# Four of sixteen scan inputs by GpSimd from broadcast rows, their decay in PSUM, and TensorE's sums behind its other jobs

## The chip, the cores and the metric

The kernel runs on one core of a Trainium2 chip. The metric is the time of one execution on the device in microseconds (us). Before the change the runs took 4894.6, 4897.47 and 4899.58 us, median 4897.47.

## The reference, cut to what matters

A layer norm, a selective state-space block with a residual, a second layer norm, and a gated feed-forward block whose activations and weights are rounded to a four-bit grid in blocks of 16. Input is 16 sequences of 1024 tokens with 256 features. The part that the change touches is the scan:

```
delta = softplus(dt_proj(dt_r) + bias)          # per head, 128 channels
A = -exp(A_log)                                 # 16 states per channel
def step(s, inp):
    d_t, u_t, B_t, C_t = inp
    dA = jnp.exp(d_t[..., None] * A)
    s = s * dA + (d_t * u_t)[..., None] * B_t[:, :, None, :]
    y_t = jnp.einsum('bhdn,bhn->bhd', s, C_t)
```

There are 4 heads with 128 channels and 16 states. B_t and C_t are the same for all channels of a head, so for each state one row of 512 tokens must be spread over 128 partitions.

## The kernel before, in words

**Tiling.** A unit is one head and 512 tokens (CH): two chunks of four heads per sequence, 128 units in all. Channels lie on the partitions and tokens along the free dimension. A unit is 16 steps, one for each state n. In units of a sequence's second chunk the scan starts from `carry`, otherwise from zero. Around the scans of unit u each step also does some job of other units: projections and convolution of units to come ("pre"), the first layer norm ("norm"), and the feed-forward part of 128-token tiles long past ("post").

**Order.** There is no planner at run time. Each engine runs `step(b, j, n)` for n = 0 to 15, and `due(job, slot)` puts a job in step slot % 16 of a unit that is slot // 16 units later than the job's start. Engines meet only through counting semaphores. Within a step the order of the code is the order of the engine's queue.

**The scan, state by state.** TensorE's `spread_b` (L904) writes the B row of state n, spread over 128 partitions, into one of three PSUM banks `db`; it does so in step n-2 and waits until the bank's last scan, three states ago, is over. VectorE multiplies the bank in place by `du` = delta*u (L840) in step n-1, ahead of the scan of state n-1, and runs the scan itself in step n (L852). ScalarE writes exp(delta*A) into the ring `decay` in SBUF (L440), five states ahead; in steps 4 and 5 it writes none and in step 6 three. GpSimd's `weigh` multiplies two states by two C rows (L629, one for each pair of states, in even steps); the C rows come from HBM by a broadcast DMA from SP's queue (`spread_c`, L383). TensorE adds the products of a pair into `ybank` and `cross` (`sum_up`, L919); the eight pairs are summed two at a time in steps 8, 12, 0 and 3 (`SUMS`).

**Jobs that the steps below name.** On TensorE: the residue matmuls L963 (step 0) and L967 (step 2), of which L963 waits for ScalarE's `hi` and `xdbl` (L553, L554, step 15); the transposes of h, L1007 (steps 13 and 0), and of v, L1051 (step 11); the gate matmuls L1026 (steps 2 and 4) and the up matmuls L993 (steps 3 and 5); the delta matmul L971 (step 4), which waits for ScalarE's `pieces` (L561); the down matmuls L1040 (steps 6, 7 and 8); the convolution L944. On ScalarE: the silu of the gate L495 (steps 3 and 5), the copy L520 of v's transpose (step 12), softplus L569 (step 5), the magnitude of h, L513 and L516 (steps 5 and 6), and table loads around silu and softplus. On VectorE: the gate product `gated` (L797, steps 4 and 6), the rounding of h, L787 and L790 (steps 6 and 7). On GpSimd: du (L655) in step 8, for the next unit.

**What of a step's queue order matters.** In each step TensorE runs the spread, then `sum_up`, then `side`, which holds all other jobs:

```python
                if g.within(STEPS):
                    spread_b(b, g)
                for slot, pairs in SUMS.items():
                    if w := due("scan", slot):
                        sum_up(w, pairs)
                side(b, u, due)
```

Of the kernel before, what the change touches and what calls it, by code (L numbers as in the profile page):

```python
# [52 lines left out]
AHEAD = RING - 1  # L53

DB_BANKS = 3
DB_BANK = [i % DB_BANKS for i in range(TRIP)]
DB_AGO = [next(d for d in range(1, TRIP) if DB_BANK[i - d] == DB_BANK[i]) for i in range(TRIP)]

# [4 lines left out]
C_RING = 4  # L63
# [68 lines left out]
def build(nc, hidden, win_t, conv_w, conv_b, xw, dtw, dt_b, a_log, dskip, wo_t, w_gate, w_up, w_down,  # L132
# [4 lines left out]
    with ExitStack() as ctx:  # L137
# [34 lines left out]
        cs = sb("cs", [C_RING, 2, CH])  # L172
        prod = sb("prod", [P_RING, 2, CH])
# [60 lines left out]
        c_landed = [sem(f"c_landed{i}") for i in range(C_RING)]  # L234
        decayed = sem("decayed")
        db_done = sem("db_done")
# [59 lines left out]
        c_rows = nc.dram_tensor("c_rows", (2, NST, CH), F32, kind="Internal").ap()  # L296

# [51 lines left out]
        def _(sp):  # L349
# [21 lines left out]
            free_reg = sp.alloc_register("free_count")  # L371
            rows_reg = sp.alloc_register("rows_count")

            def spread_c(b, u, p):

                slot = p % C_RING
                free = held(sp, free_reg, u.val(PAIRS, p + 1 - C_RING))
                if p == 0:
                    rows_in = held(sp, rows_reg, u.val(16, 16))
                    wait(sp, c_written, rows_in)  # L380
                wait(sp, weighted, free)
                rows = c_rows[u.mod(2), 2 * p:2 * p + 2, :].rearrange("n c -> (n c)")
                sp.dma_start(cs[:, slot, :, :].rearrange("p n c -> p (n c)"),  # L383
                             rows.unsqueeze(0).broadcast_to([P, 2 * CH])).then_inc(c_landed[slot], 16)

            def step(b, j, n):
                u, due = timetable(b, j, n)
                if v := due("pre", 18):
                    wait(sp, xd_evac, v.val(2, 2))
                    sp.dma_start(c_rows[v.mod(2), :, :], xdbl[64:64 + NST, :]).then_inc(c_written, 16)  # L390
                if n % 2:
                    p = (n + 5) // 2
                    w = u + p // PAIRS
                    if w.within(UNITS):
                        spread_c(b, w, p % PAIRS)
                if n == 2:
                    t_r = u + -4
                    if t_r.within(TILES):
                        wait(sp, x1_done, t_r.val(plus=-1))
                        sp.dma_start(xres[:, t_r.mod(2), :], x_tiles[t_r.val()]).then_inc(ld_res[t_r.mod(2)], 16)  # L400
                if n == 15:
                    t_x = u + 8
                    if t_x.within(TILES):
                        wait(sp, xn_done, t_x.val(plus=-1))
                        sp.dma_start(xin[:, t_x.mod(2), :], x_tiles[t_x.val()]).then_inc(ld_x[t_x.mod(2)], 16)
                    t_o = u + -8
                    if t_o.within(TILES):
                        wait(sp, o_done, t_o.val(plus=1))
                        sp.dma_start(out_tiles[t_o.val()], ot[:, t_o.mod(2), :]).then_inc(ot_free[t_o.mod(2)], 16)
# [14 lines left out]
        def _(act):  # L424
# [7 lines left out]
            def decays(b, j, n):  # L432
                g = Ix(b, j * NST + n, TRIP)
                if not g.within(STEPS):
                    return
                gu, gn = g.k // NST, g.k % NST
                if gn == 0:
                    wait(act, delta_done, Ix(b, gu, PER).val(plus=1))
                wait(act, scanned, g.val(plus=1 - RING))
                act.activation(decay[:, g.val() % RING, :], delta[:, gu % 2, :], ACT.Exp,  # L440
                               scale=aneg[:, gu % HEADS, gn:gn + 1]).then_inc(decayed, 1)

            def step(b, j, n):
                u, due = timetable(b, j, n)
                if t := due("norm", 19):
                    wait(act, xn_tp, t.val(plus=1))
                    wait(act, z_mm, t.div(4, 4, -4))
                    i = t.mod(4)
                    act.activation(xnt[:, t.mod(8) // 4, :, i * P:(i + 1) * P],
                                   bank_b[:, 0:DM].rearrange("p (k t) -> p k t", k=KM),  # L450
                                   ACT.Copy).then_inc(xnt_done, 1)
# [96 lines left out]
                if v := due("pre", 15):  # L548
                    wait(act, xd_mm, v.val(plus=1))
                    wait(act, dt_mm, v.val())  # L550
                    wait(act, res_mm, v.val(2))
                    wait(act, c_written, v.val(16))
                    act.activation(hi[:, :], pbank[:, :], ACT.Copy).then_inc(xd_evac, 1)  # L553
                    act.activation(xdbl[:, :], pbank[:, :], ACT.Copy).then_inc(xd_evac, 1)  # L554
# [3 lines left out]
                if v := due("pre", 19):  # L558
                    wait(act, res_mm, v.val(2, 2))
                    wait(act, b_spread, v.val(NST, -NST))  # L560
# [44 lines left out]
        def _(pool):  # L605
# [16 lines left out]

            def weigh(w, p):

                c, r = p % C_RING, p % P_RING
                wait(pool, scanned, w.val(NST, 2 * p + 2))
                wait(pool, c_landed[c], w.val(16 * PAIRS // C_RING, 16 * (p // C_RING + 1)))
# [4 lines left out]
            def step(b, j, n):  # L632
# [18 lines left out]
                if v := due("pre", 24):  # L651
                    wait(pool, delta_done, v.val(plus=1))
                    wait(pool, u_done, v.val(plus=1))
                    wait(pool, db_done, v.val(NST, -NST))
# [6 lines left out]
                if t := due("post", 46):  # L661
# [33 lines left out]
        def _(dve):  # L695
# [129 lines left out]
            def step(b, j, n):  # L825
# [8 lines left out]
                if g1.within(STEPS):  # L834
                    gu, gn = g1.k // NST, g1.k % NST
                    if gn == 0:
                        wait(dve, du_done, Ix(b, gu, PER).val(plus=1))
                    wait(dve, b_spread, g1.val(plus=1))
                    t = db[DB_BANK[g1.k % TRIP]]
# [3 lines left out]
                if g.within(STEPS):  # L843
                    h = u.mod(HEADS)
                    late = u.mod(PER) >= HEADS
                    wait(dve, decayed, g.val(plus=1))
                    wait(dve, db_done, g.val(plus=1))
# [4 lines left out]
                    dve.tensor_tensor_scan(state[:, n, :], decay[:, g.val() % RING, :], db[DB_BANK[g.k % TRIP]][:, :], start,  # L852
                                           ALU.mult, ALU.add).then_inc(scanned, 1)
# [29 lines left out]
        def _(pe):  # L883
# [3 lines left out]
            def step(b, j, n):  # L887
                u, due = timetable(b, j, n)
                g = Ix(b, j * NST + n + 2, TRIP)
                gu, gn = g.k // NST, g.k % NST  # L890
                if g.within(STEPS):
                    spread_b(b, g)
# [3 lines left out]
                side(b, u, due)  # L896

            def spread_b(b, g):

                gu, gn = g.k // NST, g.k % NST  # L900
                if gn == 0:
                    wait(pe, pieces_done, Ix(b, gu, PER).val(plus=1))
                wait(pe, scanned, g.val(plus=1 - DB_AGO[g.k % TRIP]))
                pe.matmul(db[DB_BANK[g.k % TRIP]][:, :], sel[:, gn, :], pieces[:, gu % 2, :],  # L904
                          start=True, stop=True).then_inc(b_spread, 1)
# [268 lines left out]
```

## Time and profile before

| | before |
|---|---|
| median of 3 runs | 4897.47 us (4894.6 to 4899.58) |
| the profiled execution | 4895.54 us, its span 4893.5 us |
| VectorE busy | 4549.8 us, 93% |
| TensorE busy (matmul) | 4234.6 us, 87% |
| ScalarE busy | 3509.2 us, 72% |
| GpSimd busy | 3429.2 us, 70% |
| spread matmuls L904 on TensorE | 690.1 us busy in the trace |
| products db*du L840 on VectorE | 1392.0 us, 2048 of them |
| scans L852 on VectorE | 2525.0 us, 2048 of them |

The times come from one profiled execution. A busy time adds up durations, and on VectorE and ScalarE the next instruction starts about 0.1 us before the one ahead is recorded as ended; where a step is priced, the distance from start to start is what counts. Matmul ends are modelled.

### The profile page before, as it was taken

How to read it: one execution, taken by the hardware profiler on the slowest of the kernel's cores; microseconds unless marked ns; L12 is line 12 of the kernel's file. 1: busy time of each engine (PE TensorE's matmuls, PEld its weight loads, DVE VectorE, ACT ScalarE, POOL GpSimd, SP SyncE). 2: the span in 40 equal slices, each digit the busy share in tenths (PEclk: the TensorE clock that was granted, in tenths of full speed). 3: DMA queues.
4: the chain of work that ended last, by engine and by line, in shares of the span. 5: the costliest groups of instructions: out<-in, count | busy, mean ns of one | idle time of the engine just before them, and what ended most of it. 6: DMA issues, size and time to landing. Idle time of an engine off the chain costs nothing. (4 is left out here: it accounts for less than half of the span.)

```text
span 4893.5 us, 64416 instructions
## 1 busy us (share of the span) xinstructions
PE 4234.6 (87%) x18927; PEld 1986.9 (41%) x19244; DVE 4549.8 (93%) x6828; ACT 3509.2 (72%) x5783; POOL 3429.2 (70%) x2321
## 2 busy tenths in 40 slices
PE   4788888888888888888898888888888888888887
PEld 1234444444444444444444444444444444444434
DVE  6999999999999999999999999999999999999994
ACT  3777777677777777777777777777777777777763
POOL 4777777777776777777777677777777677677763
PEclk8999999999999999999999999999999999999999
DMA  2333333333333333333333333333333333333330
GB/s 89 140 135 123 127 129 125 121 132 126 120 133 124 123 129 129 123 123 134 119 127 131 122 126 127 127 123 130 126 120 133 124 123 129 129 123 123 129 117 19
DMA packets 211138, 600.59 MB, mean 123 GB/s; under 512 B 25446, under 2 KB 76774, under 8 KB 210790
## 3 DMA queue, kind: packets, MB, share of 16 engines
q1 hardware_dynamic: 209088, 594.30, 35.6%
q8 instruction: 156, 2.56, 0.2%
q10 hardware_dynamic: 1702, 2.16, 0.2%
q14 instruction: 192, 1.57, 0.1%
HBM read 575.39 MB, written 20.97 MB: 122 GB/s over the span
## 5 line engine op out<-in xcount | busy, mean ns | idle before, releaser
L629 POOL TENSOR_TENSOR prod<-state,cs 128x1024 f32<-128x1024 f32 x1024 | 2416.5, 2360 | 1320.8 <-DVE state L852 1295.2
L440 ACT ACTIVATE decay<-delta,aneg 128x512 f32<-128x512 f32 x2048 | 1432.6, 717 | 925.3 <-DVE state L852 916.7
L840 DVE TENSOR_TENSOR db<-db,du 128x512 f32<-128x512 f32 x2048 | 1392.0, 680 | 56.7 <-PE db L904 55.5
L852 DVE TENSOR_TENSOR_SCAN state<-decay,carry,db 128x512 f32<-128x512 f32 x1024 | 1292.4, 1262 | 0.0
L852 DVE TENSOR_TENSOR_SCAN state<-decay,db 128x512 f32<-128x512 f32 x1024 | 1232.6, 1204 | 0.0
L904 PE MATMUL db<-pieces,sel 128*128 128x512 bf16 x1798 | 690.1, 386 | 393.5 <-DVE state L852 384.6
L919 PE MATMUL ybank<-prod,ident 64*64 64x512 f32 x4096 | 1003.4, 608 | 28.0 <-DVE hh L790 27.0
L919 PE MATMUL cross<-prod,ident 64*64 64x512 f32 x4096 | 1003.1, 609 | 0.0
L904 PEld LDWEIGHTS db<-pieces,sel 128*128 128x128 bf16 x2048 | 197.8, 97 | 1039.9 <-DVE state L852 809.0
L919 PEld LDWEIGHTS ybank<-prod,ident 64*64 64x64 f32 x4096 | 255.8, 134 | 455.1 <-issue 417.8
L1040 PE MATMUL bank_a<-wd,ht 128*128 128x256 f32 x1536 | 406.0, 389 | 3.2 <-DVE state L852 2.0
L1040 PEld LDWEIGHTS bank_a<-wd,ht 128*128 128x128 f32 x1536 | 283.1, 191 | 235.0 <-issue 210.8
L930 PE MATMUL pbank<-xnt,win 128*128 128x512 f32 x512 | 277.0, 624 | 103.7 <-ACT delta L569 64.1
L993 PE MATMUL bank_b<-wu,vt 128*128 128x352 f32 x1024 | 357.8, 472 | 0.0
L1026 PE MATMUL bank_a<-wg,vt 128*128 128x352 f32 x1024 | 347.4, 462 | 1.5 <-ACT hh L495 0.9
L797 DVE TENSOR_TENSOR hh<-hh,bank_b 128x352 f32<-128x352 f32 x256 | 132.5, 518 | 210.4 <-PE bank_b L993 203.1
L495 ACT ACTIVATE hh<-bank_a 128x352 f32<-128x352 f32 x256 | 118.6, 463 | 227.1 <-PE bank_a L1026 225.6
L1063 PE MATMUL bank_a<-wo,yg 128*128 128x256 f32 x1024 | 272.1, 391 | 0.4 <-ACT sz L546 0.3
L993 PEld LDWEIGHTS bank_b<-wu,vt 128*128 128x128 f32 x1024 | 184.3, 189 | 216.2 <-issue 160.0
L930 PE MATMUL bank_a<-xnt,win 128*128 128x512 f32 x512 | 261.0, 591 | 0.0
L944 PE MATMUL pbank<-xearly,cdiag 128*128 128x512 f32 x512 | 253.5, 598 | 3.4 <-ACT halo L531 1.5
L944 PE MATMUL pbank<-xlate,cdiag 128*128 128x512 f32 x512 | 251.1, 592 | 2.2 <-issue 0.5
(124 smaller groups left out, 6399.6 us busy)
## 6 DMA issues: line engine op xcount, KB each, us to landing
cs<-c_rows SPq DMA_DIRECT2D x1024, 512.0 KB, 3.6
xin<-in_hidden SPq DMA_DIRECT2D x128, 128.0 KB, 3.6
xres<-in_hidden SPq DMA_DIRECT2D x128, 128.0 KB, 3.4
out_x<-ot SPq DMA_DIRECT2D x128, 128.0 KB, 3.6
c_rows<-xdbl SPq DMA_DIRECT2D x128, 32.0 KB, 3.6
win<-in_win_t SPq DMA_DIRECT2D x1, 1024.0 KB, 10.6
state<-in_w_gate ACTq DMA_DIRECT2D x1, 704.0 KB
state<-in_w_up ACTq DMA_DIRECT2D x1, 704.0 KB
```

Source lines behind the costliest of these rows:

```text
L440: act.activation(decay[:, g.val() % RING, :], delta[:, gu % 2, :], ACT.Exp, scale=aneg[:, gu % HEADS, gn:gn + 1]).then_inc(decayed, 1)
L629: pool.tensor_tensor(prod[:, r, :, :], state[:, 2 * p:2 * p + 2, :], cs[:, c, :, :], ALU.mult).then_inc(weighted, 1)
L840: dve.tensor_tensor(t[:, :], t[:, :], du[:, gu % 2, :], ALU.mult).then_inc(db_done, 1)
L852: dve.tensor_tensor_scan(state[:, n, :], decay[:, g.val() % RING, :], db[DB_BANK[g.k % TRIP]][:, :], start, ALU.mult, ALU.add).then_inc(sc ...
L904: pe.matmul(db[DB_BANK[g.k % TRIP]][:, :], sel[:, gn, :], pieces[:, gu % 2, :], start=True, stop=True).then_inc(b_spread, 1)
L919: last = pe.matmul((ybank, cross)[k][c * Q:(c + 1) * Q, :], ident[rows, rows], prod[rows, p % P_RING, k, :], start=(p == 0), stop=(k == 1 ...
L930: return pe.matmul((pbank, bank_a)[part][:, :], win[:, k, part * DI + h * P:part * DI + (h + 1) * P], xnt[:, v.mod(8) // 4, k, :], start=( ...
L944: last = pe.matmul(pbank[:, :], cdiag[:, v.mod(HEADS), k, :], x[:, k:k + CH], start=(k == 0), stop=(k == TAPS - 1))
L993: last = pe.matmul(bank_b[:, 0:HALF], vt[:, k, :], wu[:, k, part * HALF:(part + 1) * HALF], start=(k == 0), stop=(k == KM - 1))
L1026: last = pe.matmul(bank_a[:, 0:HALF], vt[:, k, :], wg[:, k, part * HALF:(part + 1) * HALF], start=(k == 0), stop=(k == KM - 1))
L1040: last = pe.matmul(bank_a[:, 0:DM], ht[:, k, :], wd[:, k, :], start=(k == 0), stop=(k == KI - 1))
L1063: last = pe.matmul(bank_a[:, 0:DM], yg[:, t.mod(8) // 4, h, i * P:(i + 1) * P], wo[:, h, :], start=(h == 0), stop=(h == HEADS - 1))
```

## The change

- For states 1, 5, 9 and 13 (`BY_POOL`) the B row doesn't go over TensorE and PSUM. `xdbl`'s B rows are stored to HBM as `b_rows`, beside the C rows; SP's queue copies each of the four rows by a broadcast DMA into one of two buffers `brow` in SBUF (`copy_b`, steps 10, 14, 2 and 6); GpSimd multiplies it in place by du (`drive`, steps 15, 1, 5 and 11).
- For these states ScalarE writes the decay into the PSUM bank that TensorE doesn't use then, two states ahead, in place of the ring; the scan reads its factor from PSUM and its addend from SBUF. The other twelve states keep the old way, with a decay ring of six that runs six states ahead.
- TensorE's step is now spread, side, sums.
- The ring of C rows has three buffers, not four, and `spread_c` runs one pair less ahead.
- GpSimd computes du in step 13, not 8, and scales h (L664) in step 3, not step 14 of the unit before.

The core of the diff:

```diff
-AHEAD = RING - 1
+AHEAD = 6
+BY_POOL = (1, 5, 9, 13)
+WEIGHED_ROWS = 2
-C_RING = 4
+C_RING = 3
+            def copy_b(u, n):
+                g = u.val(NST, n)
+                i = of_pool(g)
+                if n == BY_POOL[0]:
+                    wait(sp, b_written, u.val(16, 16))
+                if i >= WEIGHED_ROWS:
+                    wait(sp, scanned, ON_POOL[i - WEIGHED_ROWS] + 1)
+                row = b_rows[u.mod(2), n:n + 1, :]
+                sp.dma_start(brow[:, i % WEIGHED_ROWS, :], row.broadcast_to([P, CH])).then_inc(b_landed[i % WEIGHED_ROWS], 16)
...
+                    sp.dma_start(b_rows[v.mod(2), :, :], xdbl[0:NST, :]).then_inc(b_written, 16)
...
+                for slot, k in ((10, 1), (14, 5), (18, 9), (22, 13)):
+                    if n == slot % NST:
+                        w = u + (1 - slot // NST)
+                        if w.within(UNITS):
+                            copy_b(w, k)
...
-                wait(act, scanned, g.val(plus=1 - RING))
-                act.activation(decay[:, g.val() % RING, :], delta[:, gu % 2, :], ACT.Exp,
-                               scale=aneg[:, gu % HEADS, gn:gn + 1]).then_inc(decayed, 1)
+                if gn in BY_POOL:
+                    wait(act, scanned, g.val(plus=1 - DB_BANKS))
+                    out, done = db[g.val() % DB_BANKS][:, :], decayed_psum
+                else:
+                    i = of_dve(g.val())
+                    if i >= RING:
+                        wait(act, scanned, ON_DVE[i - RING] + 1)
+                    out, done = decay[:, i % RING, :], decayed
+                act.activation(out, delta[:, gu % 2, :], ACT.Exp,
+                               scale=aneg[:, gu % HEADS, gn:gn + 1]).then_inc(done, 1)
...
+                if (n + 2) % NST in BY_POOL:
+                    decays(b, j, n + 2)
                 if n not in (4, 5):
                     for ahead in (AHEAD - 2, AHEAD - 1, AHEAD) if n == 6 else (AHEAD,):
-                        decays(b, j, n + ahead)
+                        if (n + ahead) % NST not in BY_POOL:
+                            decays(b, j, n + ahead)
...
+            def drive(w, n):
+                g = w.val(NST, n)
+                i = of_pool(g)
+                s = i % WEIGHED_ROWS
+                wait(pool, b_landed[s], 16 * (i // WEIGHED_ROWS + 1))
+                wait(pool, du_done, w.val(plus=1))
+                pool.tensor_tensor(brow[:, s, :], brow[:, s, :], du[:, w.mod(2), :], ALU.mult).then_inc(db_pool, 1)
...
-                if v := due("pre", 24):
+                if v := due("pre", 29):
...
+                for slot, k in ((-1, 1), (1, 5), (5, 9), (11, 13)):
+                    if w := due("scan", slot):
+                        drive(w, k)
-                if t := due("post", 46):
+                if t := due("post", 51):
...
+                    if n in BY_POOL:
+                        i = of_pool(g.val())
+                        wait(dve, decayed_psum, i + 1)
+                        wait(dve, db_pool, i + 1)
+                        by, plus = bank_g, brow[:, i % WEIGHED_ROWS, :]
...
-                if g.within(STEPS):
-                    spread_b(b, g)
+                if g.within(STEPS) and g.val() % NST not in BY_POOL:
+                    spread_b(g.val())
+                side(b, u, due)
                 for slot, pairs in SUMS.items():
                     if w := due("scan", slot):
                         sum_up(w, pairs)
-                side(b, u, due)
```

## Rows read from the trace of the kernel before

**Rows 1.** The page: busy time by engine, and TensorE's granted clock by slice.
```profile
PE 4234.6 (87%) x18927; PEld 1986.9 (41%) x19244; DVE 4549.8 (93%) x6828; ACT 3509.2 (72%) x5783; POOL 3429.2 (70%) x2321
...
PEclk8999999999999999999999999999999999999999
```

**Rows 2.** Groups of instructions by line: busy us, mean ns, idle before, releaser.
```profile
L840 DVE TENSOR_TENSOR db<-db,du 128x512 f32<-128x512 f32 x2048 | 1392.0, 680 | 56.7 <-PE db L904 55.5 <-remote 0.6
...
L655 POOL TENSOR_TENSOR du<-delta,uu 128x512 f32<-128x512 f32 x128 | 162.8, 1272 | 18.3 <-ACT delta L569 18.3
...
L508 ACT ACTIVATE bank_b<-v 128x256 f32<-128x256 f32 x128 | 47.1, 368 | 0.0
```

**Rows 3.** One line of the kernel, L748: count, durations, first and last start.
```profile
L748 DVE SCALAR_TENSOR_TENSOR yg<-uu,dsk,ybank x128: 733/739/747, 141.4 to 4793.1; 128x512 f32<-128x512 f32 x128
```

**Rows 4.** Timeline of VectorE, first and second half: start us, duration, line, [idle before].
```profile
2171.40 0.67 DVE L840 TENSOR_TENSOR db<-db,du 128x512 f32<-128x512 f32 x1
...
2175.29 0.52 DVE L797 TENSOR_TENSOR hh<-hh,bank_b 128x352 f32<-128x352 f32 x1 [1.50 <-PE bank_b L993]
...
2184.01 0.53 DVE L787 SCALAR_TENSOR_TENSOR hw<-cross,hh 128x352 f32<-128x352 bf16 x1 [0.21 <-ACT cross L516]
...
2185.58 0.50 DVE L790 SCALAR_TENSOR_TENSOR hh<-cross,hw 128x352 f32<-128x352 bf16 x1
...
2205.91 0.67 DVE L840 TENSOR_TENSOR db<-db,du 128x512 f32<-128x512 f32 x1
2206.50 0.17 DVE L744 BATCH_NORM_AGGREGATE mv<-stats 128x2 f32<-128x6 f32 x1
...
2207.69 0.67 DVE L840 TENSOR_TENSOR db<-db,du 128x512 f32<-128x512 f32 x1
...
2035.93 0.50 DVE L790 SCALAR_TENSOR_TENSOR hh<-cross,hw 128x352 f32<-128x352 bf16 x1
...
2058.67 0.67 DVE L840 TENSOR_TENSOR db<-db,du 128x512 f32<-128x512 f32 x1
```

**Rows 5.** Timeline of ScalarE in the same first-half unit.
```profile
2171.52 0.72 ACT L440 ACTIVATE decay<-delta,aneg 128x512 f32<-128x512 f32 x1 [0.51 <-DVE state L852]
...
2173.95 0.46 ACT L495 ACTIVATE hh<-bank_a 128x352 f32<-128x352 f32 x1
...
2177.55 0.46 ACT L495 ACTIVATE hh<-bank_a 128x352 f32<-128x352 f32 x1 [1.76 <-PE bank_a L1026]
...
2183.53 0.45 ACT L516 ACTIVATE cross<-hh 128x352 f32<-128x352 f32 x1
...
2195.40 0.38 ACT L520 ACTIVATE vt<-bank_b 128x256 f32<-128x256 f32 x1
...
2203.08 0.58 ACT L554 ACTIVATE xdbl<-pbank 128x512 f32<-128x512 f32 x1
```

**Rows 6.** Timeline of TensorE in that unit, neighbours of one line merged (xN).
```profile
2185.72 0.39 PE L904 MATMUL db<-pieces,sel 128*128 128x512 bf16 x1 [0.78 <-DVE state L852]
2186.34 0.65 PE L919 MATMUL ybank<-prod,ident 64*64 64x512 f32 x2 [0.23 <-DVE hh L790]
...
2188.21 1.13 PE L1040 MATMUL bank_a<-wd,ht 128*128 128x256 f32 x4
2189.18 0.38 PE L904 MATMUL db<-pieces,sel 128*128 128x512 bf16 x1
2189.40 2.95 PE L944 MATMUL pbank<-xearly,cdiag 128*128 128x512 f32 x6
...
2194.98 0.38 PE L1051 MATMUL bank_b<-ident,v 128*128 128x128 f32 x2
...
2204.41 0.49 PE L1007 MATMUL bank_b<-ident,hh 128*128 128x128 f32 x3 [0.16 <-issue]
2204.73 0.38 PE L904 MATMUL db<-pieces,sel 128*128 128x512 bf16 x1
```

**Rows 7.** DMA issues: count, KB each, median us to landing.
```profile
cs<-c_rows SPq DMA_DIRECT2D x1024, 512.0 KB, 3.6
```

More of the change, by code:

```diff
@@ L52, with of_dve, of_pool @@
 RING = 6
-AHEAD = RING - 1
+AHEAD = 6
 DB_BANKS = 3
-DB_BANK = [i % DB_BANKS for i in range(TRIP)]
-DB_AGO = [next(d for d in range(1, TRIP) if DB_BANK[i - d] == DB_BANK[i]) for i in range(TRIP)]
+BY_POOL = (1, 5, 9, 13)
+N_POOL = len(BY_POOL)
+N_DVE = NST - N_POOL
+WEIGHED_ROWS = 2
+ON_DVE = [g for g in range(STEPS) if g % NST not in BY_POOL]
+ON_POOL = [g for g in range(STEPS) if g % NST in BY_POOL]
+def of_dve(g):
+    return g // NST * N_DVE + sum(n not in BY_POOL for n in range(g % NST))
+def of_pool(g):
+    return g // NST * N_POOL + sum(n in BY_POOL for n in range(g % NST))
 PAIRS = NST // 2
-C_RING = 4
+C_RING = 3
 P_RING = 4
@@ L234, in build @@
         c_landed = [sem(f"c_landed{i}") for i in range(C_RING)]
+        b_written = sem("b_written")
+        b_landed = [sem(f"b_landed{i}") for i in range(WEIGHED_ROWS)]
+        db_pool = sem("db_pool")
         decayed = sem("decayed")
+        decayed_psum = sem("decayed_psum")
         db_done = sem("db_done")
@@ L833, in step @@
                 g1 = Ix(b, j * NST + n + 1, TRIP)
-                if g1.within(STEPS):
-                    gu, gn = g1.k // NST, g1.k % NST
+                if g1.within(STEPS) and g1.val() % NST not in BY_POOL:
+                    gu, gn = g1.val() // NST, g1.val() % NST
                     if gn == 0:
-                        wait(dve, du_done, Ix(b, gu, PER).val(plus=1))
-                    wait(dve, b_spread, g1.val(plus=1))
-                    t = db[DB_BANK[g1.k % TRIP]]
+                        wait(dve, du_done, gu + 1)
+                    wait(dve, b_spread, of_dve(g1.val()) + 1)
+                    t = db[g1.val() % DB_BANKS]
                     dve.tensor_tensor(t[:, :], t[:, :], du[:, gu % 2, :], ALU.mult).then_inc(db_done, 1)
@@ L851, in step @@
                     start = carry[:, h, n:n + 1] if late else 0.0
-                    dve.tensor_tensor_scan(state[:, n, :], decay[:, g.val() % RING, :], db[DB_BANK[g.k % TRIP]][:, :], start,
-                                           ALU.mult, ALU.add).then_inc(scanned, 1)
+                    dve.tensor_tensor_scan(state[:, n, :], by, plus, start, ALU.mult, ALU.add).then_inc(scanned, 1)
                 behind(b, j, n, due)
@@ L895, in step, with spread_b @@
                         sum_up(w, pairs)
[L896 to L900 removed]
+            def spread_b(g):
+                gu, gn = g // NST, g % NST
                 if gn == 0:
[L902 to L904 removed]
+                    wait(pe, pieces_done, gu + 1)
+                wait(pe, scanned, g + 1 - DB_BANKS)
+                pe.matmul(db[g % DB_BANKS][:, :], sel[:, gn, :], pieces[:, gu % 2, :],
                           start=True, stop=True).then_inc(b_spread, 1)
```

46 lines of the change are left out of this document (25 added, 21 removed).

## The prediction

> **What bounds the kernel now.** I read the busy shares first: VectorE is busy 93% of the span, TensorE 87%, GpSimd and ScalarE near 70% [rows 1]. So VectorE's work is what the change must shorten. Then the spacing of one instruction that runs once per unit (512 tokens of one head, 16 states): it starts 128 times from 141.4 to 4793.1 us, so a unit takes 4651.7/127 = 36.63 us, and 128 of them make nearly the whole span [rows 3]. The reader should see that anything worth x us per unit is worth 128x.
>
> Then one unit on each engine, in order of time. Two marks cut it. A is where VectorE starts the instruction behind scan 2, B where it starts the one behind scan 7. In the unit shown A is 2171.40, B is 2185.58, the next A 2207.69 [rows 4]: 14.18 us from A to B, 22.11 from B to A. In a unit of the second half of a sequence, whose scans are 0.06 longer, B to A is 22.74 [rows 4]. The two stretches have different limits:
>
> A to B is no VectorE stretch. VectorE waits 1.50 us before the first gate product (L797) and 0.21 before the rounding of the second half of h (L787) [rows 4]. What holds it is a chain over ScalarE and TensorE: the decay at 2171.52 waited for scan 2, and behind it in ScalarE's queue stand a table load and the first silu, which ends 3.0 us after A; ScalarE then waits 1.76 us for TensorE's second gate matmul; behind that silu come the softplus with its loads, three decays and the magnitude of h (L516), which ends at 2183.98, and L787 starts at 2184.01 [rows 4, 5]. That chain starts at scan 2 and ends in the step of scan 7.
>
> B to A is VectorE's own work without a gap. The waits of others on VectorE there cost nothing now.
>
> **The change, part by part.**
>
> Four of sixteen products db*du leave VectorE, those of states 1, 5, 9 and 13. One is 0.68 us long, but the next instruction starts 0.59 after it (2205.91 to 2206.50) [rows 2, 4], so 0.59 is the price: 4 x 0.59 = 2.36 us per unit, 302 us in all, if nothing else holds. State 5 lies in A to B, the three others in B to A.
>
> The product of state 5 (A to B): its place is just ahead of the gate product, where VectorE waits anyway. The gate product now also needs TensorE's up matmul, which the new order puts ahead of the sums, so it comes 1.9 us sooner; but it needs the first silu too, which ends 3.0 after A as before. VectorE saves some 0.8 us there and then stands before L787, because L516 comes when it did: the decay of state 5 replaces that of state 8 in the same place of ScalarE's queue, with the same wait for scan 2, and the three decays ahead of L516 stay three. Gain in A to B: nothing, 14.18 stays. The sums of pairs 6 and 7, now behind the up matmul, are followed by the delta matmul, which waits for ScalarE's pieces longer than for them.
>
> B to A: VectorE alone would need 22.11 - 3 x 0.59 = 20.34 in early units and 20.97 in late ones. It would reach the product of state 3 1.78 earlier (2205.91 to 2207.69), at B + 18.56 and B + 19.19 [rows 4]. That product needs TensorE's spread of state 3, and here the second edit bites. In step 0 TensorE now does the residue matmul (L963) and the h transposes (L1007) first and the sums of pairs 4 and 5 behind them; the spread of state 3 is step 1's first instruction, behind the sums. L963 waits for ScalarE's xdbl. Before, the sums covered that wait. When xdbl comes, from B:
> - TensorE's first spread at 0.14; then the down matmul without the wait for the rounding (L1040 is now ahead of the sums), so the block of work starts 0.32 after the spread, not 0.62 [rows 6].
> - From the sums to the transpose L1051 8.64, whatever the order inside, less one spread that is gone: 0.22 (2189.18 to 2189.40) [rows 6]: 8.42.
> - L1051 to ScalarE's copy L520 0.42; from L520 to the end of xdbl 8.26, ScalarE without a gap (2195.40 to 2203.66) [rows 5, 6]. It keeps the same number of decays (state 1's is among them now).
> Sum 0.14 + 0.32 + 8.42 + 0.42 + 8.26 = 17.56. Then L963 0.26 behind its releaser (as the first sums stand 0.26 behind the end of L790, 2186.08) and 0.22 long, L1007 0.32 plus 0.08 of turnover, the sums 1.87 (2186.34 to 2188.21), and the spread, whose result VectorE can take 0.43 after its start (0.38 and 0.05) [rows 4, 6]: 17.56 + 0.26 + 0.22 + 0.40 + 1.87 + 0.43 = 20.74. VectorE would be there at 18.56 to 19.19: it waits 1.6 to 2.2 us. A follows at 20.74 + 1.78 = 22.52.
>
> So the new unit is 14.18 + 22.52 = 36.70 us (36.73 with the longer scans at the end), against 36.63: +0.1 x 128 = +13 us. VectorE's 2.36 us turn into waits.
>
> GpSimd gets four products of 128x512 per unit; its like, du, takes 1.27 us [rows 2]. 3429.2/128 = 26.8 us per unit become 31.9 of 36.7 [rows 1]. They are issued two to four states before use; the nearest to the edge is du itself, moved five steps later (from step 8 to 13, behind a weighing) and needed in step 15. I take nothing for it: VectorE has 1.6 us to give in B to A before a late du counts. GpSimd's h product moves from step 14 to 3, two steps before its user on ScalarE; nothing. SP's queue gets four broadcasts and one store more; each waits for a scan and behind it stand the C rows. A broadcast lands in 3.6 us with 512 KB [rows 7], a B row has 256 KB and is issued at least four steps before its use, and the C ring of three still leaves two weighings between issue and use. The price is zero, at the worst a late row.
>
> The four scans read their factor from PSUM and the addend from SBUF, the reverse of now: still one of each. No row has this form. Between nothing and some 0.1 each, hidden by the waits named. The decays into PSUM: ScalarE's write of 128x256 into PSUM takes 0.37 us, a read from PSUM into SBUF 0.38 [rows 2, 5]; I take no difference; ends -0.1 and +0.1 for each of the two on the chain, 26 us in all either way.
> The Trainium skill says otherwise (ScalarE: Activation LUTs, Step-by-step: what each stage is for): ScalarE writes PSUM faster than SBUF. It gives no figure; at an estimated 0.1 for the two decays on the chain the time would be 26 us lower, 4882. The rows neither confirm nor exclude it.
> Against the change stands the page GPSIMD Engine Reference, section Engine selection: elementwise products belong on VectorE, as GpSimd is about half as fast. The trace agrees (1.27 against 0.68), but GpSimd has the room.
>
> The profiled execution took 4895.54 us, span 4893.5, the median of the runs is 4897.47. The sum: 4895.5 + 13 = 4908 us.
>
> **The rivals.**
>
> Cover stays (faster). If TensorE gets xdbl 1.6 to 2.2 us sooner than in my sum, or a link of it is shorter, the spread of state 3 is in time and B to A is VectorE's: mean 20.66, unit 34.84, against the 36.61 of the two units shown: -1.77 x 128 = -227, 4669 us. For it: VectorE is 93% busy. Against it: both ends of ScalarE's 8.26 are in the trace, and no edit shortens it. Partly true cases lie between, 13 us for each 0.1. Chance 0.22.
>
> Both stretches free (faster). With the 1.7 us of waits in A to B gone too: 33.1, some 4450 us. ScalarE's chain speaks against it. Chance 0.02.
>
> TensorE's clock falls (slower). The new waits, 1.6 us and more before L963, join those it has. The granted clock is at 0.9 or more in all slices but the first with 13% of the span idle [rows 1], so waits up to now do not lower it. If each new one did, at half the clock the sums alone, on the chain, cost 1.87 more: +239, 5147 us. The Trainium skill (TensorE: Matmul & The Clock Gate, HAM oscillation) describes such a kernel; this trace does not show it. Chance 0.05.
>
> GpSimd or a row late (slower). It decides once du or a B row is over 1.6 us behind VectorE; every microsecond beyond is 128 us: one gives 5036. Chance 0.09.
>
> **How the numbers follow.** Forecast 0.62, own range 4863 to 4953 (0.35 us per unit either way on 14.18 + 22.52). This kernel's measurement tells 0.2%, 10 us, from no change; of the 0.62, 0.14 lies over 10 us below, 0.16 within, 0.32 above. With the rivals: faster 0.14 + 0.22 + 0.02 = 0.38, same 0.16, slower 0.32 + 0.05 + 0.09 = 0.46. The range takes most of the partly covered cases and leaves the ends: 4700 to 4960.
>
> **What would show it.** Right: VectorE waits once per unit for the spread (L904) before the product of state 3, by 1.6 to 2.2 us; TensorE or its weight loads wait for xdbl before L963 with the sums behind; A to B stays near 14.2 with waits at L797 and L787; VectorE's busy share falls to 88%. Wrong: no wait before state 3 and a unit near 35 us (the chain was over-counted); waits of scans for a decay or a GpSimd product; scans of another length; a granted clock below 0.9.

## Result and the profile after

The changed kernel takes 4957.86 us, the median of its runs (4955.71 to 4960.81), against 4898.52 for the kernel before on the same chip: ratio 1.0121 [1.0103, 1.0138], slower by 1.2%. The profiled execution took 4960.81 us, its span is 4958.7. One of four executions of e1 below took 16708 us and one of e2 6762 us, each far from its other three, which lie within 8 us of each other; the medians given count them.

| | before | after |
|---|---|---|
| profiled execution, us | 4895.54 | 4960.81 |
| VectorE busy | 4549.8, 93% | 4279.3, 86% |
| TensorE busy (matmul) | 4234.6, 87% | 4191.1, 85% |
| ScalarE busy | 3509.2, 72% | 3455.7, 70% |
| GpSimd busy | 3429.2, 70% | 4055.5, 82% |
| a unit, from start to start of one line | 36.63 | (4853.7 - 138.3)/127 = 37.13 |

VectorE lost 270 us of work and the kernel became 59 us longer. The page of the kernel after: its busy line and the row of the granted clock (tenths of full speed in 40 slices), then groups by line (busy us, mean ns of one, idle before and who ended it), last a DMA group (count, KB, us to landing).

```profile
PE 4191.1 (85%) x18416; PEld 1974.0 (40%) x18732; DVE 4279.3 (86%) x6316; ACT 3455.7 (70%) x5783; POOL 4055.5 (82%) x2833
...
PEclk8999999999999999999999999999999999999998
...
L899 DVE TENSOR_TENSOR db<-db,du 128x512 f32<-128x512 f32 x1536 | 1047.2, 682 | 344.1 <-PE db L970 186.4
...
L481 ACT ACTIVATE decay<-delta,aneg 128x512 f32<-128x512 f32 x1536 | 1061.5, 716 | 78.8 <-DVE state L920 75.7
...
L481 ACT ACTIVATE db<-delta,aneg 128x512 f32<-128x512 f32 x512 | 350.0, 684 | 610.3 <-DVE state L920 610.2
...
L675 POOL TENSOR_TENSOR brow<-brow,du 128x512 f32<-128x512 f32 x512 | 651.3, 1272 | 0.0
...
L920 DVE TENSOR_TENSOR_SCAN state<-db,carry,brow 128x512 f32<-128x512 f32 x256 | 325.6, 1272 | 0.0
L920 DVE TENSOR_TENSOR_SCAN state<-db,brow 128x512 f32<-128x512 f32 x256 | 310.2, 1212 | 1.7 <-ACT db L481 1.7
...
brow<-b_rows SPq DMA_DIRECT2D x512, 256.0 KB, 3.6
```

Read the idle column. The products db*du (L840 before, L899 now) had 56.7 us of idle ahead of them [rows 2] and have 344.1: that is where VectorE's saving went. The scans of the four moved states have 0.0 and 1.7: no scan waits for GpSimd or for a row, and only one of 512, by 1.7 us, for a decay in PSUM. The granted clock still stands at 9 in nearly every slice, and this row hides something, as will be seen.

The marks are those of the prediction: A behind scan 2, B behind scan 7. Means over 113 units of the run, the first 13 and the last two left out: A to B 14.22 before and 13.97 after, B to A 22.68 and 23.50. VectorE's timeline of one unit after, then of the B to A of the next (start us, duration, line, in brackets the idle ahead and who ended it):

```profile
2168.99 0.50 DVE L849 SCALAR_TENSOR_TENSOR hh<-cross,hw 128x352 f32<-128x352 bf16 x1
...
2191.28 0.70 DVE L899 TENSOR_TENSOR db<-db,du 128x512 f32<-128x512 f32 x1 [3.31 <-PE db L970]
...
2193.08 0.67 DVE L899 TENSOR_TENSOR db<-db,du 128x512 f32<-128x512 f32 x1
...
2196.20 0.52 DVE L856 TENSOR_TENSOR hh<-hh,bank_b 128x352 f32<-128x352 f32 x1 [1.33 <-ACT hh L539]
...
2207.02 0.50 DVE L849 SCALAR_TENSOR_TENSOR hh<-cross,hw 128x352 f32<-128x352 bf16 x1
...
2244.99 0.50 DVE L849 SCALAR_TENSOR_TENSOR hh<-cross,hw 128x352 f32<-128x352 bf16 x1
...
2265.59 0.70 DVE L899 TENSOR_TENSOR db<-db,du 128x512 f32<-128x512 f32 x1 [1.62 <-PE db L970]
...
2267.39 0.68 DVE L899 TENSOR_TENSOR db<-db,du 128x512 f32<-128x512 f32 x1
```

The first B is 2168.99, A 2193.08: 24.09, with a wait of 3.31 before the product of state 3. The next B is 2207.02, so A to B is 13.94. In the other unit B is 2244.99 and A 2267.39: 22.40, with a wait of 1.62. [Rows 4] has no wait there. So there are two kinds of unit, and TensorE's timeline of both shows why. First the long one, then the short one:

```profile
2186.53 0.39 PE L1029 MATMUL pbank<-hi,less 128*128 128x512 bf16 x1 [1.59 <-ACT xdbl L599]
...
2187.18 1.06 PE L985 MATMUL ybank<-prod,ident 64*64 64x512 f32 x2
...
2189.73 1.07 PE L985 MATMUL ybank<-prod,ident 64*64 64x512 f32 x2
...
2190.75 0.60 PE L970 MATMUL db<-pieces,sel 128*128 128x512 bf16 x2
...
2262.53 0.39 PE L1029 MATMUL pbank<-hi,less 128*128 128x512 bf16 x1 [1.60 <-ACT xdbl L599]
...
2263.18 0.65 PE L985 MATMUL ybank<-prod,ident 64*64 64x512 f32 x2
...
2264.52 0.60 PE L985 MATMUL ybank<-prod,ident 64*64 64x512 f32 x2
...
2265.06 0.60 PE L970 MATMUL db<-pieces,sel 128*128 128x512 bf16 x2
```

And the busy times of these two stretches (us, then busy time and count of PE, PEld, DVE, ACT and POOL, granted clock, DMA share, GB/s):

```profile
2186.50:2191.00 4.50, 4.47 (x22) 1.37 (x23) 1.47 (x3) 2.78 (x6) 3.63 (x3) 0.62 0.73 243
2262.50:2267.00 4.50, 4.46 (x29) 2.29 (x30) 2.88 (x6) 3.16 (x7) 4.45 (x4) 1.00 0.75 238
```

Both units wait 1.6 us before L1029 (L963 before). In the second the clock stays at 1.00, the last row of sums starts 1.34 us behind the first, and the spread L970 follows. In the first the mean clock of the stretch is 0.62, since part of it ran at the lower level of 1.2 GHz (1.00 is 2.4 GHz); the last row of sums starts 2.55 us behind the first, one row takes 1.06 us where it took 0.65, and the spread comes 4.22 us behind L1029, not 2.53. 76 of the 113 units are of the long kind (mean B to A 24.07, the others 22.34). The mean of 0.62 is one of 4.50 us in a unit of 38, so the clock's row of the page hardly moves; what gives it away is one line's matmuls with two durations.

### The profile page after: what moved, and what is told of

Its sections match the earlier page's. It is cut to its first block and busy times, and to the rows that moved or that the text cites. A ratio compares the mean times of both kernels' runs of the same rounds, so it can differ in the third digit from the quotient of the medians.

```text
span 4958.7 us, 64797 instructions
## 1 busy us (share of the span) xinstructions
PE 4191.1 (85%) x18416; PEld 1974.0 (40%) x18732; DVE 4279.3 (86%) x6316; ACT 3455.7 (70%) x5783; POOL 4055.5 (82%) x2833
## 5 line engine op out<-in xcount | busy, mean ns | idle before, releaser
L899 DVE TENSOR_TENSOR db<-db,du 128x512 f32<-128x512 f32 x1536 | 1047.2, 682 | 344.1 <-PE db L970 186.4
L481 ACT ACTIVATE decay<-delta,aneg 128x512 f32<-128x512 f32 x1536 | 1061.5, 716 | 78.8 <-DVE state L920 75.7
L920 DVE TENSOR_TENSOR_SCAN state<-decay,carry,db 128x512 f32<-128x512 f32 x768 | 963.2, 1260 | 0.0
L920 DVE TENSOR_TENSOR_SCAN state<-decay,db 128x512 f32<-128x512 f32 x768 | 918.7, 1203 | 0.1
L481 ACT ACTIVATE db<-delta,aneg 128x512 f32<-128x512 f32 x512 | 350.0, 684 | 610.3 <-DVE state L920 610.2
L970 PE MATMUL db<-pieces,sel 128*128 128x512 bf16 x1224 | 462.6, 387 | 246.0 <-DVE state L920 234.0
L675 POOL TENSOR_TENSOR brow<-brow,du 128x512 f32<-128x512 f32 x512 | 651.3, 1272 | 0.0
L970 PEld LDWEIGHTS db<-pieces,sel 128*128 128x128 bf16 x1536 | 139.1, 97 | 1000.8 <-DVE state L920 534.8
L1059 PE MATMUL bank_b<-wu,vt 128*128 128x352 f32 x1024 | 344.7, 459 | 0.0
L920 DVE TENSOR_TENSOR_SCAN state<-db,carry,brow 128x512 f32<-128x512 f32 x256 | 325.6, 1272 | 0.0
L920 DVE TENSOR_TENSOR_SCAN state<-db,brow 128x512 f32<-128x512 f32 x256 | 310.2, 1212 | 1.7 <-ACT db L481 1.7
L985 PEld LDWEIGHTS cross<-prod,ident 64*64 64x64 f32 x4096 | 265.1, 144 | 0.0
```

Source lines behind the costliest of these rows:

```text
L481: act.activation(out, delta[:, gu % 2, :], ACT.Exp, scale=aneg[:, gu % HEADS, gn:gn + 1]).then_inc(done, 1)
L675: pool.tensor_tensor(brow[:, s, :], brow[:, s, :], du[:, w.mod(2), :], ALU.mult).then_inc(db_pool, 1)
L899: dve.tensor_tensor(t[:, :], t[:, :], du[:, gu % 2, :], ALU.mult).then_inc(db_done, 1)
L920: dve.tensor_tensor_scan(state[:, n, :], by, plus, start, ALU.mult, ALU.add).then_inc(scanned, 1)
L970: pe.matmul(db[g % DB_BANKS][:, :], sel[:, gn, :], pieces[:, gu % 2, :], start=True, stop=True).then_inc(b_spread, 1)
L985: last = pe.matmul((ybank, cross)[k][c * Q:(c + 1) * Q, :], ident[rows, rows], prod[rows, p % P_RING, k, :], start=(p == 0), stop=(k == 1 ...
```

## Experiments

The first four kernels cut the change by its parts.

**e1_old_order**: the four products go to GpSimd, but TensorE keeps its old order.

```diff
-                side(b, u, due)
                 for slot, pairs in SUMS.items():
                     if w := due("scan", slot):
                         sum_up(w, pairs)
+                side(b, u, due)
```

> The changed kernel with TensorE's old order in every step: spread, sums, then the other jobs. Theory (the wait for xdbl, put ahead of the sums of step 0, holds the product of state 3): the wait before that product goes, from 2.5 us on average in the changed kernel to nothing; from mark B to mark A is VectorE's own 20.3 to 21.0 us, from A to B near 14.2 again, a unit about 35.1 where the kernel before needs 36.9 in its middle: about 4680 us. TensorE stays at full clock in step 0. Rival (GpSimd, now 82% busy, or the broadcast rows hold the scans, and the order of the sums is beside the point): the wait before state 3 goes but others take its place, and the time stays above 4850 us.

Measured 4810.55 us, 0.9826 [0.981, 0.9842]. There is no wait before the product of state 3 any more, so the new order makes it. But the gain is 84 us of 302, 130 us short of what was expected, and both stretches keep something (A to B is 14.49 in the mean, B to A 21.80). VectorE around A:

```profile
2198.01 0.68 DVE L899 TENSOR_TENSOR db<-db,du 128x512 f32<-128x512 f32 x1
...
2202.43 0.52 DVE L856 TENSOR_TENSOR hh<-hh,bank_b 128x352 f32<-128x352 f32 x1 [2.63 <-PE bank_b L1059]
```

TensorE in the step of scan 8:

```profile
2177.96 0.65 PE L985 MATMUL ybank<-prod,ident 64*64 64x512 f32 x2 [2.14 <-DVE hh L849]
```

The gate product stands 4.42 us behind A and waits for the up matmul (L1059), which the old order puts behind sums: the second edit had a use, in step 3. And TensorE waits 2.14 us for VectorE before the sums of step 8. In half of the units this wait is 2.1 to 2.3 us; in the others TensorE waits 1.5 to 1.6 us before the spread just ahead of them and 0.2 more before the sums. In 55 of 113 units the clock drops behind these waits, 27 of them of the first kind and 28 of the second (B to A 22.67 against 20.97).

**e2_step0_first** and **e7_step0_again** are one kernel: the change, with the old order in step 0 only. All rows are those of the second.

```diff
+                if n == 0:
+                    for slot, pairs in SUMS.items():
+                        if w := due("scan", slot):
+                            sum_up(w, pairs)
                 side(b, u, due)
-                for slot, pairs in SUMS.items():
-                    if w := due("scan", slot):
-                        sum_up(w, pairs)
+                if n != 0:
+                    for slot, pairs in SUMS.items():
+                        if w := due("scan", slot):
+                            sum_up(w, pairs)
```

> The changed kernel with the sums ahead of the other jobs in step 0 alone; in steps 3, 8 and 12 they stay behind. Theory (only step 0 costs): as the full old order or a little less, since the up matmul of step 3 comes ahead of the sums and from A to B is near 13.97 as in the changed kernel, not 14.18: about 4660 us. Rival (the sums behind the jobs cost in the other steps too): clearly slower than the full old order, by 0.5 us per unit or more, over 4740 us.

> The kernel with the old order in step 0 alone once more, for a profile at full clock. Theory: 4670 us again; from B to A VectorE works without a gap, 20.3 to 21.0 us, from A to B near 14.0 with its waits before L797 and L787; TensorE's clock stays up in nearly all units, a unit about 34.7 us. Rival: part of the gain comes from something else than the product of state 3, and a wait before it stays.

Measured 4670.51 us, 0.9543 [0.9527, 0.9559], and 4671.15 us, 0.9546 [0.9532, 0.9561]. One step's order is worth 287 us, and this kernel beats both, the one before by 223 us. The busy line of its page:

```profile
PE 4059.7 (87%) x18416; PEld 1936.0 (41%) x18732; DVE 4270.1 (91%) x6316; ACT 3466.2 (74%) x5783; POOL 4043.6 (87%) x2833
```

VectorE from state 3 to B:

```profile
2171.11 0.67 DVE L899 TENSOR_TENSOR db<-db,du 128x512 f32<-128x512 f32 x1
...
2172.95 0.68 DVE L899 TENSOR_TENSOR db<-db,du 128x512 f32<-128x512 f32 x1
...
2176.06 0.52 DVE L856 TENSOR_TENSOR hh<-hh,bank_b 128x352 f32<-128x352 f32 x1 [1.26 <-ACT hh L539]
...
2187.21 0.50 DVE L849 SCALAR_TENSOR_TENSOR hh<-cross,hw 128x352 f32<-128x352 bf16 x1
```

TensorE around A and behind B:

```profile
2171.85 0.39 PE L1038 MATMUL pbank<-mid,less 128*128 128x512 bf16 x1 [0.20 <-ACT mid L602]
...
2176.64 0.39 PE L975 MATMUL db<-pieces,sel 128*128 128x512 bf16 x1
2176.87 1.02 PE L1042 MATMUL pbank<-xdbl,dtws 128*128 128x512 f32 x2
...
2187.58 1.03 PE L1111 MATMUL bank_a<-wd,ht 128*128 128x256 f32 x4 [1.82 <-DVE state L920]
```

The product of state 3 starts without a wait. A to B is 2172.95 to 2187.21, 14.26 (14.21 in the mean, where 14.0 was expected): the stretch that the products do not shorten. B to A is 20.87 in the mean of the 113 units, none of them long.

**e3_order_alone**: the kernel before, with the new order of TensorE in all steps (the same move as above, the other way).

> The kernel before with one edit: TensorE's other jobs ahead of the sums in every step. All sixteen products stay on VectorE. Theory (the order alone makes the chain from scan 7 over TensorE, ScalarE's xdbl, L963 and the sums to the spread of state 3): VectorE waits 1.5 to 3 us before the product of state 3 although it has more work, TensorE idles over 1 us before L963 and its clock drops in part of the units; from B to A 22.6 us at full clock and some 24.3 where the clock drops; slower than before by 0.5 to 1.0 us per unit: 4960 to 5020 us. Rival (the order only hurts together with GpSimd's products or the decays in PSUM): within 10 us of the kernel before, 4890 to 4910 us.

Measured 4946.95 us, 1.0109 [1.0092, 1.0126]: 52 us slower, with no product moved. TensorE before L963:

```profile
2184.74 0.39 PE L963 MATMUL pbank<-hi,less 128*128 128x512 bf16 x1 [1.31 <-ACT xdbl L554]
```

VectorE's product of state 3:

```profile
2187.80 0.70 DVE L840 TENSOR_TENSOR db<-db,du 128x512 f32<-128x512 f32 x1 [0.74 <-remote]
```

The wait at the product is here too, 0.54 us in the mean, with VectorE's full load. So the chain over L963 is longer than VectorE's own stretch in either kernel, and the products moved off VectorE only make the wait longer: 1.42 in the mean at full clock (e5 below), 2.52 in the change with its drops of the clock. Here B to A is 23.26 in the mean. The clock did not drop behind the waits before L963, which are 1.10 to 1.32 us in 95 of the 113 units, where it had been expected to. It did drop in 7 of the 113 units behind another wait, one of 2.82 us before a spread that comes in one unit of eight (14 of 113); the kernel before has a like one, of which more below.

**e9_order_but_step0**: the kernel before, new order in steps 3, 8 and 12 alone (the diff of e2, on the kernel before).

> The kernel before with the sums behind TensorE's other jobs in steps 3, 8 and 12 alone; no product is moved. It fills the table of parts: products moved with the old order 4810, the order alone in all steps 4947, both but for step 0 4671. Theory: VectorE has its full work from B to A, 22.1 to 22.7 us, and A to B goes from 14.18 to 13.97: about 25 us faster than before, 4870; so the 223 us of the good version are more than the sum of its parts (84 and 25), because the old order leaves A to B to TensorE and the clock once VectorE is fast. Rival (the two parts just add): this kernel takes about 4755 us.

Measured 4885.77 us, 0.9979 [0.9969, 0.9989], against 4895.46 for the kernel before beside it: 10 us faster, so in step 0 the order costs 52 + 10 = 62 us and elsewhere it gains a little, while VectorE has its full load. The parts do not add up: the order but step 0 gives 10, the products 84, the two together 223. Each takes away the limit that held the other back.

**e4_fill**: the change, with 22 small matmuls ahead of L1029 to keep TensorE busy in its wait. They stood behind a condition that is never true in this kernel, so what ran is the change again.

```diff
+                if not peeled and n == 0:
+                    wait(pe, ht_done, (u + -8).val(2, 1))
+                    for _ in range(22):
+                        pe.matmul(bank_b[:, 3 * P:4 * P], sel[:, 0, :], sel[:, 1, :], start=True, stop=True)
```

> The changed kernel with 22 small bf16 matmuls (128 columns, about 1.2 us together, their result used by nobody) between the spread and L963 in step 0, so that TensorE works where it waited for xdbl; the wait itself and its place stay. Theory of two prices (the wait costs VectorE its own time, and in two units of three the granted clock halves after it and the sums of step 0 take 1.7 us more): the slow sums go, from B to A is 22.4 us in all units, a unit 36.4 in place of 37.5 in the middle: about 4835 us. Rival (the clock halves for another reason, as the load of TensorE over the whole unit): the half-clock sums stay and the time stays at 4958 us or grows.

Measured 4959.93 us, 1.0134 [1.0118, 1.0149]: it says nothing on the clock, only that the change repeats within 2 us.

**e5_fill_wait**: the same with 13 matmuls that do stand in the queue (0.90 us of work, not the 1.2 expected). They write a part of bank_b that nothing reads.

```diff
+                if t := due("post", 64):
+                    wait(pe, ht_done, t.val(2, 1))
+                    for _ in range(13):
+                        pe.matmul(bank_b[:, 3 * P:4 * P], sel[:, 0, :], sel[:, 1, :], start=True, stop=True)
```

> The changed kernel with 13 small bf16 matmuls (128 columns, about 1.2 us together, their result used by nobody) between the spread and L963 in step 0, this time really in the queue of every unit, so that TensorE works for most of its wait for xdbl; the wait for xdbl itself stays where it is. Theory of two prices (the wait costs VectorE its own time, and in two units of three the clock halves behind it and the sums of step 0 take 1.7 us more): the half-clock sums go, from B to A is 22.4 us in all units and a unit 36.4, 1.1 less than the mean of the changed kernel: about 4830 us. Rival (the clock halves for the load of the whole unit, whatever fills the wait): half-clock sums stay in two units of three, 4958 us or more.

Measured 4824.59 us, 0.9859 [0.9842, 0.9875]: work that is good for nothing makes the kernel 133 us faster than the change. TensorE's timeline:

```profile
2163.64 0.90 PE L1030 MATMUL bank_b<-sel 128*128 128x128 bf16 x13
...
2165.22 0.39 PE L1033 MATMUL pbank<-hi,less 128*128 128x512 bf16 x1 [0.68 <-ACT xdbl L599]
...
2165.86 0.65 PE L985 MATMUL ybank<-prod,ident 64*64 64x512 f32 x2
```

The fillers leave 0.68 us of the wait, the sums keep 0.65, and no unit has a B to A of 24. The wait before the product of state 3 is still there, 1.42 us in the mean, and B to A is 22.40. So two costs are apart: the drops of the clock, 4957.86 - 4824.59 = 133 us, and the order of step 0 at full clock, 4824.59 - 4671.15 = 153 us. The second is a net figure: in e7 B to A is 1.53 shorter than here and A to B 0.24 longer.

**e6_only_step3**: the change, sums behind the side work in step 3 only (the diff of e2 with 3 in place of "not 0").

> The changed kernel with the sums behind the other jobs in step 3 alone; steps 0, 8 and 12 have the old order. It parts the 140 us between the full old order (4810) and the old order in step 0 alone (4670). If step 3 is worth it all (the up matmul ahead of the sums shortens A to B): about 4670. If step 8 is worth part of it (in the old order TensorE waits there for the rounding of h and its clock drops afterwards in part of the units): A to B falls from 14.49 to 13.97 us, worth some 60 us, the half-clock stretches stay, about 4750 us. My theory is the second.

Measured 4789.12 us, 0.9786 [0.9771, 0.98]: 118 us slower than e7, though only steps 8 and 12 differ. TensorE at the sums of step 8 in a long unit, where the wait is a long one as in e1:

```profile
2095.41 0.94 PE L990 MATMUL ybank<-prod,ident 64*64 64x512 f32 x2 [2.14 <-DVE hh L849]
```

The windows behind that wait in this unit and in a short one (columns as above, the clock third from the end):

```profile
2095.40:2098.40 3.00, 2.99 (x16) 0.86 (x16) 2.92 (x4) 1.19 (x3) 2.92 (x4) 0.54 0.02 10
2169.50:2172.50 3.00, 2.96 (x21) 1.49 (x22) 2.95 (x4) 1.27 (x3) 2.92 (x4) 1.00 0.07 23
```

48 of 113 units are long (22.70 against 20.96), (48/113) x 1.74 x 128 = 95 us of the 118; A to B, longer by 0.19, makes 24. Of the 48, 22 have the wait of 2.1 to 2.3 us before the sums, 26 the one of 1.5 to 1.6 us before the spread and 0.2 more. With the down matmul (L1111) ahead of the sums the waits in that step are 1.5 to 1.6 us before the spread or 1.7 to 1.8 before L1111, and e7 has no long unit. The drops start within 3 us of B; that is why they are put down to step 8, which no run parts from step 12.

**e8_centre_first**: e7, with ScalarE's centring of v ahead of the decay of state 5, so that the first silu (L539) has one instruction less between scan 2 and itself.

```diff
+                if t := due("post", 19):
+                    wait(act, st2, t.val(2, 2))
+                    wait(act, v_tp, t.val())
+                    act.activation(v2[:, :], x1[:, t.mod(4), :], ACT.Identity, bias=mv2[:, 0:1],
+                                   scale=-1.0).then_inc(centred2, 1)
                 if (n + 2) % NST in BY_POOL:
                     decays(b, j, n + 2)
```

(its old place, behind the silu's block, goes away)

> The best kernel so far (changed kernel, old order in step 0 alone, 4671 us), and in ScalarE's step 3 the centring of the second layer norm (0.40 us) stands ahead of the decay of state 5 that waits for scan 2, not behind it. It tests what bounds A to B. Theory (a ScalarE chain that starts at scan 2): the chain behind that decay is 0.40 us shorter, the first silu ends 2.6 us after A and not 3.0, A to B falls from 14.0 to about 13.6 us: some 45 us less, 4625. Rival (TensorE's row of gate, up, sums and delta matmuls sets A to B): the silu comes sooner, but the second gate matmul and the magnitude of h do not, less than 15 us.

Measured 4668.05 us, 0.9539 [0.9525, 0.9553]: nothing. A is 2174.16 in this trace. VectorE's gate product, then ScalarE's two silus, then TensorE's delta and second gate matmul:

```profile
2176.94 0.52 DVE L856 TENSOR_TENSOR hh<-hh,bank_b 128x352 f32<-128x352 f32 x1 [0.93 <-ACT hh L539]
```

```profile
2176.37 0.47 ACT L539 ACTIVATE hh<-bank_a 128x352 f32<-128x352 f32 x1
...
2180.31 0.47 ACT L539 ACTIVATE hh<-bank_a 128x352 f32<-128x352 f32 x1 [1.74 <-PE bank_a L1097]
```

```profile
2178.06 1.02 PE L1042 MATMUL pbank<-xdbl,dtws 128*128 128x512 f32 x2
2178.92 1.35 PE L1097 MATMUL bank_a<-wg,vt 128*128 128x352 f32 x4
```

The first silu starts 2.21 us behind A and the gate product 2.78 (3.11 in e7), so the move did what it says. But the second silu waits for TensorE, whose delta matmul (L1042) starts 3.90 behind A as in e7 (2172.95 to 2176.87, 3.92). The mean A to B is 14.22, and 14.21 in e7. In e7 and e8 TensorE runs without a gap from L1038, about 1.1 us ahead of A, to the second gate matmul, and this row of matmuls sets A to B, not ScalarE's first silu. What starts the row is ScalarE again: L1038 waited 0.20 us for its copy `mid` (L602), which comes out of the chain before A.

## Why the prediction was right, and where not

The forecast was 4908 us and "slower"; measured were 4957.86 and slower, 2 us inside the upper end of the range (4960) and 5 us above the forecast's own range of 4863 to 4953. The mechanism of the wait was right; that the time came out inside the range was in part luck, as the base and the clock below show.

**The products.** The price of 2.36 us of VectorE's time per unit held: its busy time fell by 270 us, and it came back as idle before the products.

**A to B.** "14.18 stays": measured 13.94 and 13.97. The reasons given were half of it. The delta matmul did wait for ScalarE's pieces (0.60 us before L1037), but started 3.56 us behind A where before it had started 3.90 behind it with no wait, since up and sums were done sooner; this is the 0.2 us. e8 shows that where TensorE has no such wait its own row of work sets this stretch: I had named both engines and put the start of the chain on ScalarE.

```profile
2196.64 1.13 PE L1037 MATMUL pbank<-xdbl,dtws 128*128 128x512 f32 x2 [0.60 <-ACT pieces L606]
```

**B to A, the chain.** The forecast was 22.52 with a wait of 1.6 to 2.2 before the product of state 3. In units at full clock it measured 22.40 in the mean (e5) and 22.34 (the change), with waits of 1.25 to 1.64 in all but four; both means are 22.43 without the four short units at the end. The links hold: ScalarE's copy to the end of xdbl took 8.26 again, and e3, e7 and e5 show the cause and the price. In the following rows xdbl ends at 2186.47 and the copy began at 2178.21. One link was too long: L963 was put 0.26 behind the end of xdbl, and L1029 starts at 2186.53, 0.06 behind it.

```profile
2178.21 0.39 ACT L564 ACTIVATE vt<-bank_b 128x256 f32<-128x256 f32 x1 [1.80 <-PE bank_b L1117]
...
2185.89 0.58 ACT L599 ACTIVATE xdbl<-pbank 128x512 f32<-128x512 f32 x1
```

**"Cover stays" (0.22).** It did not happen, but its sum, 4669 us, is near the time of e7 (4671.15), the kernel in which the cover was put back. That it is so near is partly chance: its unit of 34.84 measured 20.87 + 14.21 = 35.08, and its base of 36.61 measured 36.90; the two errors, 0.24 and 0.29 us, cancel.

**The base.** The unit of the forecast, 36.70, is one from the middle of the run, and I set it against 36.63, the spacing over the whole run. The like quantity before is 14.22 + 22.68 = 36.90: the mean of B to A is that high because 14 of 113 units (one in eight) have 24.59 where the others have 22.41, and neither of the units I had read [rows 4] was such a one. Against 36.90 the forecast would have been -0.20 x 128 = -26 us. Without the drops of the clock the change measured 4824.59 - 4894.45 = -70 us; the 44 us between are the two stretches, each shorter than in the sum (13.97 for 14.18, 22.40 for 22.52). About half of the 70, (14/113) x 2.18 x 128 = 35 us, is that the changed kernel no longer has the long unit in eight, which the prediction didn't see; why it is gone no run shows. So my +13 was right in sign only by the term that follows.

**The clock (0.05): the step that failed.** I had written that waits up to now don't lower the clock and took the new one of 1.6 us as no exception. It lowered it in 76 of 113 units, and the long units are 24.07 - 22.34 = 1.73 us longer, near the rival's 1.87; 133 us by e5. The rival priced it in every unit (239 us) and gave it one chance in twenty; the likeliest case should have carried part of it. The premise was wrong too, and the trace of the kernel before could have told it: the drop is in it. The long unit in eight has a wait of 2.64 us on TensorE, and in 7 of the 14 the clock drops behind it (B to A near 25.0, against 24.17 in the other seven). TensorE in the unit from 2109.76, and the window behind the wait:

```profile
2124.93 0.38 PE L904 MATMUL db<-pieces,sel 128*128 128x512 bf16 x1 [2.64 <-DVE state L852]
...
2125.57 1.80 PE L1069 MATMUL pbank<-uu,xws 128*128 128x512 f32 x2
2127.34 0.61 PE L904 MATMUL db<-pieces,sel 128*128 128x512 bf16 x1
```

```profile
2126.00:2130.00 4.00, 4.00 (x10) 1.85 (x8) 3.19 (x5) 2.93 (x7) 3.14 (x2) 0.61 0.62 197
```

TensorE waits 2.64 us for a scan, over the window behind it the mean clock is 0.61, the xdbl matmul takes 1.80 where it takes 1.02 elsewhere, and the spread 0.61 for 0.38. This comes every 590 us, too seldom and too short for the digits of the clock's row [rows 1] to fall, so I took these digits for the absence of drops. The forecast came out near because errors cancelled: the low base (39 us) and the two stretches (44 us) made it too high by 83, the clock that was left out made it too low by 133; 50 us remain, which is what 4957.86 lies above 4908. The Trainium skill (TensorE: Matmul & The Clock Gate, HAM oscillation) describes kernels whose TensorE falls back to the lower clock after its waits, time and again; its main example has waits for DMA of 3 to 5 us. The trace agrees, in two units of three, and here behind waits of 1.6 us and less.

**GpSimd and the rows (0.09).** Wrong: GpSimd is busy 82%, 87% in e7, and no scan waits for it or for a row, which lands in 3.6 us.

**PSUM.** The scan with its factor in PSUM takes 1212 and 1272 ns, against 1203 and 1260 for the one with its addend there; a decay into PSUM 684 ns against 716 into SBUF. Both lie inside the bounds taken for them. The Trainium skill (ScalarE: Activation LUTs, Step-by-step: what each stage is for) has PSUM as the faster target; the trace agrees by 32 ns, a third of the 0.1 that I had estimated for it.

**What stays open.** Why the clock drops in one unit and not in the next: both units shown wait 1.6 us before L1029, of the 37 units at full clock 33 wait 1.36 to 1.61 us as the 76 long ones do, and the waits of 2.64 us before are all alike.

## What to carry to other kernels

Work that covers a wait of the engine behind it belongs to that wait: before it is moved behind the wait, add up the chain from the releaser to the next user and set it against the idle engine's own stretch, step by step, since here the same move was worth 10 us in three steps and cost 62 in the fourth. When a sum makes a new wait for TensorE, carry the clock's drop as a term and not as a far rival, and look for matmuls of one line with two durations, not at the average clock. Compare a forecast unit with the mean of like units before, not with the spacing over the run, and count how many units differ from the one that was read.

## What was unexpected in the hardware

- TensorE's clock fell to its lower level, a mean of 0.54 to 0.62 over stretches of 3 to 4.5 us, behind waits of 1.35 to 1.61 us (the change, 76 of 113 units), behind one of 2.1 to 2.3 us or one of 1.5 to 1.6 and 0.2 more (e1 and e6, 55 and 48 units), and behind waits of 2.64 us (the kernel before) and 2.82 us (e3, e9), in 7 of 14 units each. It did not fall behind waits of 1.10 to 1.32 us (before L963 in e3), 0.68 (e5) or 1.5 to 1.8 (at B in e7). The length of one wait alone does not decide it.
- Thirteen matmuls of 128x128 that nothing reads, 0.90 us of work per unit, took the drops away and made the kernel 133 us faster.
